# One decoder layer on one core: the next group's Gram products moved to the head of a body, the substitution moved ahead of the row scaling and scatter, and the long filter laced with the first inverse

## The chip, the cores and the metric

The kernel runs on one core of one Trainium2 chip. The metric is the device time of one execution in microseconds (us): 1143.61 is the median of three runs before the change (1141.53 to 1147.48).

## The reference

A pre-norm decoder layer in float32 over x of 4 x 1024 x 256: gated delta-rule attention, cross attention to 64 context rows, and a mixture of experts with a shared expert. Cut to what the change touches, the attention is:

```
hs = layernorm(x)
q, k, v = silu(causal_conv4(hs @ W))          # 4 heads of 64
A  = strict_lower((beta k) k^T)               # per chunk of 32 rows
u, w = inv(I + A) v, inv(I + A) (beta k)      # unit-triangular solve
for each chunk:                               # state S, 64 x 64 per head
    u = u - w S;  o = q S + lower(q k^T) u;  S = S + k^T u
short, long = fir3(v), fir31(v)
gates = softmax(gelu([hs, mean short, mean long, mean delta] W1) W2 / temp)
o = g0 short + g1 long + g2 delta + g3 v
x = x + (o * rsqrt(mean(o*o)) * w) @ Wo
x = x + cross_attention(layernorm(x), context)
x = x + moe(layernorm(x))                     # top 2 of 8 experts
```

The kernel solves blocks of 128 rows, not of 32: it inverts 32-row blocks by substitution and doubles them twice with products.

## The kernel before

The 4096 rows are eight groups of 512 (`NG`), a group four tiles of 128 (`T`), with 16 blocks of head and tile (`HT`). Each of the five engines has a program of its own, written out by hand in the order in which it runs: PE (TensorE) from L408, ACT (ScalarE) from L1033, POOL (GpSimd) from L1383, DVE (VectorE) from L1619, SP (which issues most DMAs) from L2332. Semaphores tie them together. An engine runs its queue strictly in order, so a wait holds back all that stands behind it. The eight PSUM banks go from one fill to the next: `open_bank` (L334) waits until the bank's last fill has been drained.

**Projection**: for each group PE projects six chunks, ACT evacuates them, DVE runs the four taps of the convolution (L1673) and lays v out for the long filter (`spread`, L1680).

**Long filter**: two channels of eight blocks on PE (`long_filter`, L492), ACT evacuates, DVE transposes each channel (`long_turned`, L1767) and SP stores it.

**Eight bodies** (`body`, PE L747, ACT L1239, POOL L1557, DVE L2005). Body i works on three things at once:

- the attention of group i. The inverse of its unit-triangular blocks is finished by products (`pair_inner`, L676; `pair_corner`, L687; `half_inner`, L702; `half_corner`, L713). `solved_rows` (L726) applies it, and two of the four resulting banks are copied by ACT, two by DVE (L2034). Then come the state loop (`wa`, masked by DVE at L2059 and L2063), the output loop (`outputs`), the gates (`gate_hidden`, L816, and the logits at L909, softmax on DVE from L2109), the mixing (L2137 to L2145), the output norm and the output products (L934);
- the cross attention and routing of group i-1, tagged x. DVE computes the row statistics (L1637, L1641), POOL their rstd (`norm_scale`, L1412: twice a body), DVE the normalised rows (`rows3`, L1647);
- the front of group i+1: Gram products (`front_gram` on PE, L468, a product pair for each of two banks of a tile, masked on DVE at L1722 and L1725), POOL's copies of the diagonal blocks (`front_diagonals`, L1442), DVE's transposition of them (`front_units`, L1732), POOL's substitution (`front_steps`, L1538: 31 steps, k = 31 down to 1, two operations each, L1544 and L1546), POOL's scaling of keys and values (`front_rows`, L1513 and L1516 for each tile), DVE's copies of the solved blocks (L1784, L1790).

From body 2 on, POOL also scatters the rows of group i-2 to the slots of the experts, two indirect DMAs a tile (L1489), each tile's behind the scaling of that tile. Their slots come from the positions that PE counts (`positions(i-2, 7)`, in bank 7) and DVE turns into slots (`slots`, from L1947).

POOL's order in a body is first `norm_scale`, all four tiles of `front_rows` with scatter, `front_solve` with the diagonals, and the steps, with two things between them:

```
                    if k == 18 and x is not None:
                        norm_scale(1, "x", 2 * x + 2)
                    if k == 5:
                        norm()
```

where `norm` is `output_norm` (L1558, one power of 128x8 for each half). Behind the bodies the tiles of the mixture of experts run; the change does not touch them.

## Time and profile before

| | |
|---|---|
| runs | 1143.61, 1147.48, 1141.53 us |
| the profiled execution | 1144.12 us, span 1142.3 us, mean granted clock 0.95 |
| PE busy | 997.4 us, 87% of the span |
| DVE busy | 803.6 us, 70% |
| POOL busy | 622.9 us, 55% |
| ACT busy | 528.2 us, 46% |

The span is the time from the first to the last instruction of the profiled execution; the rest of its own time lies around it. Busy is an average over stages: the projection takes until about 181 us, the long filter until about 217, the bodies from there until about 940, the tiles of the experts the rest. The granted clock is a share of TensorE's full 2.4 GHz. Rows give the start in us, the duration, the engine and its line, the operation, output and input, shapes, the count, and in brackets the idle time before it on that engine with what ended it.

### The profile page before, as it was taken

What the parts mean: (1) busy time and instruction counts of PE and PEld (TensorE: products, weight loads), DVE (VectorE), ACT (ScalarE), POOL (GpSimd) and SP (SyncE); (2) the same over time, 40 slices, a digit from 0 to 9 for tenths busy, and PEclk for the clock granted to TensorE, in tenths of its full rate; (3) what the DMA queues carried; (4) which work ended last, traced back from release to release, by engine and by line L of the source; (5) the groups of instructions that cost most, each with busy time, mean ns of one, the idle gap of its engine ahead of it and who ended that gap; (6) DMA issues with size and microseconds to landing.
All of it is one profiled execution on the core that took longest, in us unless ns stands there. A gap on an engine that the chain in (4) does not pass through costs nothing.

```text
span 1142.3 us, 26147 instructions
## 1 busy us (share of the span) xinstructions
PE 997.4 (87%) x9538; PEld 733.1 (64%) x9538; DVE 803.6 (70%) x2110; ACT 528.2 (46%) x992; POOL 622.9 (55%) x1009
## 2 busy tenths in 40 slices
PE   4899997887699899899999989989989999988991
PEld 2465657765476676576666667667667667767891
DVE  2879984543676866787677687687678775657487
ACT  2877774513333532542443443353253255755770
POOL 5469898438126636816816735653673215335562
PEclk9999998869799989999989999999999999999996
DMA  9444534450101250260161152122111173224589
GB/s 197 133 163 143 175 93 149 151 157 19 57 20 42 75 151 21 65 185 31 65 183 38 47 141 93 48 70 77 38 55 58 56 266 110 90 89 128 166 286 341
DMA packets 87100, 127.69 MB, mean 112 GB/s; under 512 B 28352, under 2 KB 62784, under 8 KB 84800
## 3 DMA queue, kind: packets, MB, share of 16 engines
q1 hardware_dynamic: 79776, 106.30, 30.2%
q0 software_dynamic: 7200, 19.74, 4.8%
q8 instruction: 78, 1.28, 0.5%
q14 instruction: 46, 0.38, 0.1%
HBM read 66.47 MB, written 59.55 MB: 110 GB/s over the span
## 4 chain that ended last, share of the span: by engine, by line
PE 45%; POOL 20%; DVE 20%; issue 8%; ACT 4%; DMA 1%; SPq 1%; ACTq 0%; DVEq 0%; POOLq 0%
POOL arena L1544 7%; POOL arena L1546 7%; DVE arena L1673 3%; PE bank L562 3%; PE bank L499 3%; PE bank L734 3%; PE bank L468 2%; PE bank L970 2%; POOL orn L1562 2%; PE bank L816 2%; POOL arena L1434 2%; PE bank L576 2%; PE bank L436 2%; PE bank L934 2%; PE bank L588 2%
## 5 line engine op out<-in xcount | busy, mean ns | idle before, releaser
L1044 ACT ACTIVATE arena<-bank 128x512 f32<-128x512 f32 (+4 forms) x358 | 185.9, 539 | 348.8 <-PE bank L961 61.8
L1544 POOL TENSOR_TENSOR arena<-arena 128x126 f32<-128x126 f32 (+22 forms) x248 | 107.0, 432 | 43.9 <-DVE arena L1732 26.1
L1673 DVE SCALAR_TENSOR_TENSOR arena<-arena,param 128x512 f32<-128x512 f32 x144 | 104.1, 777 | 18.8 <-ACT arena L1067 18.1
L1607 POOL DMA_INDIRECT results<-arena x78 | 76.3, 978 | 71.2 <-DVE arena L2225 42.9
L1546 POOL TENSOR_TENSOR arena<-arena 128x126 f32<-128x126 f32 (+22 forms) x248 | 102.2, 412 | 19.4
L419 PE MATMUL bank<-const,arena 128*128 128x128 f32 x256 | 40.5, 310 | 52.7 <-DVE arena L2162 26.7
L1489 POOL DMA_INDIRECT slots_x<-arena x64 | 63.6, 994 | 37.3 <-DVE arena L1964 21.4
L970 PE MATMUL bank<-arena 128*128 128x128 f32 x624 | 83.6, 277 | 0.2 <-ACT arena L1344 0.2
L1513 POOL TENSOR_TENSOR arena<-arena,rb 128x256 f32<-128x256 f32 x32 | 19.7, 616 | 116.5 <-ACT arena L1044 116.0
L970 PEld LDWEIGHTS bank<-arena 128*128 128x128 f32 x624 | 76.9, 194 | 0.4 <-issue 0.4
L1442 POOL COPY arena<-arena 32x128 f32<-32x128 f32 x128 | 53.5, 418 | 38.2 <-DVE arena L1722 31.4
L419 PEld LDWEIGHTS bank<-const,arena 128*128 128x128 f32 x256 | 33.2, 160 | 62.1 <-DVE arena L2162 29.7
L1722 DVE SCALAR_TENSOR_TENSOR arena<-bank,sc,const 128x128 f32<-128x128 f32 x128 | 38.5, 342 | 29.9 <-PE bank L468 29.9
L648 PE MATMUL bank<-arena 128*128 128x512 f32 x128 | 58.2, 608 | 0.0
L977 PE MATMUL bank<-arena 128*128 x156 | 49.5, 399 | 10.0 <-DVE arena L2214 9.8
L2214 DVE TENSOR_TENSOR arena<-bank,arena 128x128 f32<-128x128 f32 x78 | 22.3, 287 | 45.9 <-PE bank L970 23.6
L1854 DVE TENSOR_REDUCE top<-bank 128x8 f32<-128x512 f32 x64 | 43.8, 685 | 14.9 <-PE bank L579 14.7
L1275 ACT ACTIVATE wt<-bank 64x128 f32<-64x128 f32 x64 | 17.4, 271 | 74.0 <-PE bank L851 69.9
L1434 POOL TENSOR_SCALAR arena<-xt,mv_hs,rstd_hs 128x256 f32<-128x256 f32 x32 | 49.8, 1565 | 0.8
L1344 ACT ACTIVATE arena<-arena 128x512 f32 x78 | 48.7, 624 | 0.3
L468 PE MATMUL bank<-kq 64*128 64x256 f32 x224 | 35.5, 438 | 13.4 <-DVE arena L1725 12.3
L436 PE MATMUL bank<-hsT,wt 128*128 128x512 f32 x96 | 46.5, 628 | 0.8 <-ACT hsT L1044 0.8
(293 smaller groups left out, 2635.6 us busy)
## 6 DMA issues: line engine op xcount, KB each, us to landing
arena<-slots_x SPq DMA_DIRECT2D x78, 129.0 KB, 2.1
slots_x<-rows_of_no_token SPq DMA_DIRECT2D x8, 1161.0 KB, 11.7
xt<-x_in SPq DMA_DIRECT2D x16, 512.0 KB, 5.6
kq<-kq_T SPq DMA_DIRECT2D x8, 1024.0 KB, 9.0
arena<-results SPq DMA_DIRECT2D x32, 256.0 KB, 4.8
kq_T<-kq SPq DMA_DIRECT2D x7, 1024.0 KB, 3.9
arena<-ffn_in SPq DMA_DIRECT2D x7, 768.0 KB, 4.1
vT<-v_T SPq DMA_DIRECT2D x8, 514.0 KB, 4.0
```

What stands on the lines that cost most here:

```text
L419: last = tr(o[:, t * P:(t + 1) * P], src[:, t, c * P:(c + 1) * P], ident)
L436: last = mm(o[:, :], wgt("kqv"[j // 2], c, D)[:, (j % 2) * P:(j % 2 + 1) * P], hsT_b[i % 2][:, c, :], start=c == 0, stop=c == CK - 1)
L468: last = mm(o[r][:, c * 2 * P:(c + 1) * 2 * P], src[rr, c, 0, tt], src[rr, c, :, tt], start=True, stop=True)
L648: last = mm(o[:, :], w_[:, c, :], xnT[:, c, :], start=c == 0, stop=c == CK - 1)
L970: last = mm(o[:, s_ * P:(s_ + 1) * P], gu_w[:, n % 2, s_, c, :], xTs[:, n % 2, c, :], start=c == 0, stop=c == CK - 1)
L1044: free(act.activation(out_, in_, func, **kw), name)
L1434: done(pool.tensor_scalar(xn_hs[:, t, :], xt[:, i % G, t, :], mv[0][:, t, 0:1], rstd[0][:, t:t + 1], ALU.subtract, ALU.mult), "hs_rows_ready")
L1489: pool.indirect_dma_start(slots_x[PART[i]][:, :], bass.IndirectOffsetOnAxis(ap=slot_at[:, i * T + t, k:k + 1], axis=0), xn_f[:, t, :], Non ...
L1544: own.link(pool.tensor_tensor(tmp, rows32[:, m0:, k].unsqueeze(2).broadcast_to([P, nm, k]), units[:, 0:k, k].unsqueeze(1).broadcast_to([P, ...
L1546: ins = pool.tensor_tensor(rows32[:, m0:, 0:k], rows32[:, m0:, 0:k], tmp, ALU.subtract)
L1607: pool.indirect_dma_start(results[:, :], bass.IndirectOffsetOnAxis(ap=dest[:, n % YS:n % YS + 1], axis=0), ys[:, n % YS, :], None).then_in ...
L1673: ins = V.scalar_tensor_tensor(cv[:, k % 4, :], pre[:, j, d:d + GT], param[:, at:at + 1], cv[:, k % 4, :], ALU.mult, ALU.add)
```

## The change

- **Projection of the last group.** Its chunks run in the order 0, 4, 5, 1, 2, 3, so that v is there first; `spread(7)` follows the taps of its fifth chunk. The sums of squares of the last group move into the long filter.
- **Long filter and first inverse.** The long filter's second channel has storage of its own and uses three banks in turn. Its blocks alternate on PE and ACT with group 0's `pair_inner`, value tiles, `pair_corner`, `half_inner`, `half_corner`, and then with group 1's four Gram tiles. DVE masks those Gram tiles and transposes their units before body 0, POOL runs group 1's substitution before body 0.
- **Body 0** begins with `solved_rows(0)`. DVE's transposition of the second channel stands inside it. POOL does the output norm first and `front_rows(1)` behind it; group 1's value tiles stand at the end of PE's and ACT's body 0.
- **Bodies 1 to 6.** PE's Gram products of group i+1 stand before and behind `half_corner` (tiles 0 and 1, banks 6 and 7) and behind the second and third `wa` (tiles 2 and 3, banks 2 and 3); DVE's masks before its first scores, and behind the second and third `wa`; `front_units` behind the fourth. ACT copies all four banks of `solved_rows`.
- **POOL in bodies 1 to 6** runs diagonals and steps first. One tile of `front_rows` with its scatter follows each of the steps k = 28, 24, 20 and 16; the second `norm_scale` follows step 8 (it was 18); the output norm follows the last step (it was behind step 5).
- **SP** loads keys and queries of group i+2 in body i, the first `load_hs` earlier, and fills empty slots later; five loads of filter taps go with each group (it was four).

The core of the diff:

```diff
@@ POOL
-            def front_steps(i, x=None, norm=lambda: None):
+            ROWS_AT = (28, 24, 20, 16)
+
+            def front_steps(i, x=None, moved=None):
...
-                    if k == 18 and x is not None:
+                    if x is not None and k in ROWS_AT:
+                        front_rows(i, moved, (ROWS_AT.index(k),))
+                    if k == 8 and x is not None:
                         norm_scale(1, "x", 2 * x + 2)
-                    if k == 5:
-                        norm()
...
                 if i == 0:
-                    front_solve(1)
-                    front_steps(1)
+                    output_norm()
                     front_rows(1)
                 elif ahead:
-                    front_rows(i + 1, moved)
-                    if i >= 2:
-                        h = PART[i - 2]
-                        pool.wait_ge(sem(f"scattered{h}"), 32 * T * (i - 1 - FIRST[h]))
                     front_solve(i + 1)
-                    front_steps(i + 1, x, output_norm)
...
+                    for t in range(T):
+                        front_diagonals(i + 1, t)
+                    front_steps(i + 1, x, moved)
+                    output_norm()
@@ PE, body
                     queries()
...
+                    if ahead:
+                        keys_loaded(i + 1)
+                        next_gram(i + 1, 0, (6, 7))
+                    half_corner(i)
+                    if ahead:
+                        next_gram(i + 1, 1, (6, 7))
                     masked_scores(0)
...
                     if x and t == 1:
+                        if ahead:
+                            next_gram(i + 1, 2, (2, 3))
                         values(0)
@@ DVE, body
+                    if ahead:
+                        front_gram(i + 1, 0)
+                        front_gram(i + 1, 1)
                     scores(0)
-                    solved_rows()
...
                 if x:
+                    if ahead:
+                        filled(dve, f"edge1.{i}")
+                        front_units(i + 1)
                     scores(2)
@@ PE, ahead of body 0
+            pair_inner(0)
+            long_filter(1, 0)
+            front_values(0, 0)
+            pair_corner(0)
+            long_filter(1, 1)
...
+            for t in range(T):
+                next_gram(1, t)
                 long_filter(1, 4 + t)
```

Three places in the engines' orders, before and now. The first is POOL's queue at the head of a body before: `orn` is the output norm's result, `rstd_x` the x stream's rstd, `rb` and `sc` the factors of the scaling, the DMA is the pair of scatters of a tile, L1442 the diagonals, and the 128x31 operations the first step.

```order
L1414 TENSOR_TENSOR rstd_x<-mv_x,eps 128x4
L1415 TENSOR_TENSOR rstd_x<-rstd_x,minus_half 128x4
L1513 TENSOR_TENSOR arena<-arena,rb 128x4x64
L1516 TENSOR_TENSOR arena<-arena,sc 128x4x64
L1489 DMA slots_x<-arena 32768x258 x2
...
L1527 COPY arena<-start 128x512
L1442 COPY arena<-arena 32x32x4 x16
L1544 TENSOR_TENSOR arena<-arena 128x31
L1546 TENSOR_TENSOR arena<-arena 128x31
```

All four tiles of scaling and scatter (one shown) stood ahead of the diagonals and of the first step. Around the second rstd (behind the 128x126 step) and the output norm POOL's queue before was:

```order
L1546 TENSOR_TENSOR arena<-arena 128x7x18
L1414 TENSOR_TENSOR rstd_x<-mv_x,eps 128x4
L1415 TENSOR_TENSOR rstd_x<-rstd_x,minus_half 128x4
L1544 TENSOR_TENSOR arena<-arena 128x136
...
L1546 TENSOR_TENSOR arena<-arena 128x14x5
L1562 TENSOR_TENSOR orn<-oss,minus_half 128x8 x2
L1544 TENSOR_TENSOR arena<-arena 128x56
```

The same queue now, from the head of the body, with the first scaled tile, the rstd and the output norm.

```order
L1571 COPY arena<-start 128x512
L1486 COPY arena<-arena 32x32x4 x16
L1583 TENSOR_TENSOR arena<-arena 128x31
...
L1585 TENSOR_TENSOR arena<-arena 128x2x28
L1557 TENSOR_TENSOR arena<-arena,rb 128x4x64
L1560 TENSOR_TENSOR arena<-arena,sc 128x4x64
L1533 DMA slots_x<-arena 32768x258 x2
L1583 TENSOR_TENSOR arena<-arena 128x81
...
L1585 TENSOR_TENSOR arena<-arena 128x12x8
L1458 TENSOR_TENSOR rstd_x<-mv_x,eps 128x4
L1459 TENSOR_TENSOR rstd_x<-rstd_x,minus_half 128x4
...
L1601 TENSOR_TENSOR orn<-oss,minus_half 128x8 x2
```

The scaled tile and its scatter moved from ahead of the diagonals to between the steps, the rstd from behind the 128x126 step to behind the 128x96 step, the output norm to the end. The third place is PE's queue before, from the products of the queries (L562) to the half-corner (L723), the first scores (L576, L579) and the solved rows (L734):

```order
L562 MATMUL bank6<-arena,wt 128x512 x2
L723 MATMUL bank2<-arena 64x64 x8
L723 MATMUL bank3<-arena 64x64 x8
L576 MATMUL bank4<-arena 128x256
L576 MATMUL bank5<-arena 128x256
L576 MATMUL bank4<-arena 128x256
L576 MATMUL bank5<-arena 128x256
L579 MATMUL bank4<-mb,ident_b 128x512
L579 MATMUL bank5<-mb,ident_b 128x512
L734 MATMUL bank0<-arena 128x128 x4
```

and now, with the Gram products at L477 and the half-corner at L731:

```order
L570 MATMUL bank6<-arena,wt 128x512 x2
L477 MATMUL bank6<-kq1 128x256
L477 MATMUL bank7<-kq1 128x256
L477 MATMUL bank6<-kq1 128x256
L477 MATMUL bank7<-kq1 128x256
L731 MATMUL bank2<-arena 64x64 x8
L731 MATMUL bank3<-arena 64x64 x8
L477 MATMUL bank6<-kq1 128x256
L477 MATMUL bank7<-kq1 128x256
L477 MATMUL bank6<-kq1 128x256
L477 MATMUL bank7<-kq1 128x256
L584 MATMUL bank4<-arena 128x256
```

Two Gram tiles (four rows each) moved in, in banks 6 and 7; bank 6 holds the queries' second product just before.

## Rows read from the trace of the kernel before

**Rows 1.** The page: its first line, and the chain's shares by engine.

```profile
span 1142.3 us, 26147 instructions
...
PE 45%; POOL 20%; DVE 20%; issue 8%; ACT 4%; DMA 1%; SPq 1%; ACTq 0%; DVEq 0%; POOLq 0%
```

**Rows 2.** The timeline of POOL in body 3.

```profile
509.59 0.61 POOL L1513 TENSOR_TENSOR arena<-arena,rb 128x256 f32<-128x256 f32 x1 [17.79 <-ACT arena L1044]
...
513.32 0.62 POOL L1513 TENSOR_TENSOR arena<-arena,rb 128x256 f32<-128x256 f32 x1
...
539.27 0.25 POOL L1544 TENSOR_TENSOR arena<-arena 128x31 f32<-128x31 f32 x1 [3.92 <-DVE arena L1732]
...
552.34 0.20 POOL L1414 TENSOR_TENSOR rstd_x<-mv_x,eps 128x4 f32<-128x4 f32 x1
...
564.21 0.70 POOL L1546 TENSOR_TENSOR arena<-arena 128x96 f32<-128x96 f32 x1
...
567.81 3.23 POOL L1562 TENSOR_TENSOR orn<-oss,minus_half 128x8 f32<-128x8 f32 x2
```

**Rows 3.** The timeline of DVE in body 3.

```profile
502.24 0.18 DVE L1947 TENSOR_TENSOR arena<-bank,arena 128x32 f32<-128x32 f32 x1
...
507.41 0.69 DVE L2038 COPY arena<-bank 128x512 f32<-128x512 f32 x1 [0.20 <-PE bank L734]
...
518.26 0.57 DVE L2063 TENSOR_TENSOR wt<-const,bank 64x128 f32<-64x128 f32 x2
...
522.61 0.60 DVE L1722 SCALAR_TENSOR_TENSOR arena<-bank,sc,const 128x128 f32<-128x128 f32 x2
...
524.31 0.24 DVE L1865 RECIPROCAL rden<-bank 128x16 f32<-128x16 f32 x1
...
537.88 1.24 DVE L1732 STREAM_TRANSPOSE arena<-arena 128x1024 f32<-128x1024 f32 x1
...
553.77 2.14 DVE L1647 TENSOR_SCALAR arena<-xt,mv_x,rstd_x 128x256 f32<-128x256 f32 x4 [2.12 <-POOL rstd_x L1415]
...
574.49 1.06 DVE L1784 STREAM_TRANSPOSE arena<-arena 128x512 f32<-128x512 f32 x1 [0.35 <-POOL arena L1546]
```

**Rows 4.** The timeline of PE, from the end of body 2 to the end of body 3.

```profile
486.51 1.99 PE L934 MATMUL bank<-wt,arena 128*128 128x256 f32 x8
...
500.12 2.07 PE L723 MATMUL bank<-arena 64*64 64x64 f32 x32
...
524.53 1.13 PE L468 MATMUL bank<-kq 64*128 64x256 f32 x8 [1.14 <-DVE arena L1725]
...
578.15 1.99 PE L934 MATMUL bank<-wt,arena 128*128 128x256 f32 x8
```

**Rows 5.** The timelines of DVE and PE at the end of body 7.

```profile
916.43 1.39 DVE L1647 TENSOR_SCALAR arena<-xt,mv_x,rstd_x 128x256 f32<-128x256 f32 x4 [1.51 <-POOL rstd_x L1415]
...
935.69 3.62 PE L934 MATMUL bank<-wt,arena 128*128 128x256 f32 x16
```

**Rows 6.** The timelines of DVE and PE in bodies 0 and 1.

```profile
281.98 4.21 DVE L2141 SCALAR_TENSOR_TENSOR arena<-arena,gw 128x256 f32<-128x256 f32 x2
...
287.69 0.86 DVE L2141 SCALAR_TENSOR_TENSOR arena<-arena,gw 128x256 f32<-128x256 f32 x2
...
294.27 1.97 PE L419 MATMUL bank<-const,arena 128*128 128x128 f32 x8 [15.94 <-DVE arena L2162]
...
302.04 1.99 PE L934 MATMUL bank<-wt,arena 128*128 128x256 f32 x8
...
368.55 2.21 DVE L1647 TENSOR_SCALAR arena<-xt,mv_x,rstd_x 128x256 f32<-128x256 f32 x4 [2.02 <-POOL rstd_x L1415]
```

**Rows 7.** Windows: stretch, length, busy time by engine, PEclk, DMA share, GB/s.

```profile
496.88:518.83 21.95, 21.92 (x259) 17.17 (x259) 17.95 (x42) 8.72 (x15) 8.09 (x11) 1.00 0.46 138
217.80:245.20 27.40, 17.56 (x192) 13.75 (x192) 14.37 (x32) 7.42 (x13) 6.72 (x32) 0.53 0.73 241
294.00:301.00 7.00, 6.00 (x29) 4.44 (x31) 2.08 (x4) 3.59 (x6) 0.00 (x0) 0.50 0.01 2
```

More of the change, by code:

```diff
@@ L778, in body @@
                 for t in range(T):
-                    if ahead:
+                    if x and ahead:
                         front_values(i + 1, t)
@@ L818, in gate_hidden, with head_means @@
                         full(last, n)
-                n = f"gm.{i}"
-                o = open_bank(pe, n, next(body_bank))
-                pe.wait_ge(sem("short_done"), 2 * i + 2)
-                pe.wait_ge(sem("long_loaded"), 16 * (i + 1))
-                for c in range(CK):
-                    mm(o[0:DH, :], cst("mean_s")[:, 0:DH], sht[:, c, :], start=c == 0, stop=c == CK - 1)
-                    last = mm(o[DH:2 * DH, :], cst("mean_l")[:, DH:2 * DH], lng[:, c, :], start=c == 0, stop=c == CK - 1)
-                full(last, n)
-                if x and ahead:
-                    next_gram(i + 1, 1)
+                def head_means():
+                    n = f"gm.{i}"
+                    o = open_bank(pe, n, next(body_bank))
+                    pe.wait_ge(sem("short_done"), 2 * i + 2)
+                    pe.wait_ge(sem("long_loaded"), 16 * (i + 1))
+                    for c in range(CK):
+                        mm(o[0:DH, :], cst("mean_s")[:, 0:DH], sht[:, c, :], start=c == 0, stop=c == CK - 1)
+                        last = mm(o[DH:2 * DH, :], cst("mean_l")[:, DH:2 * DH], lng[:, c, :], start=c == 0,
+                                  stop=c == CK - 1)
+                    full(last, n)
+                if x:
+                    head_means()
                 pe.wait_ge(sem("hs_loaded"), 16 * (i + 1))
@@ L834, in body @@
                 for t in range(T):
-                    if x and ahead and t == 0:
-                        next_gram(i + 1, 2)
                     drained(pe, f"wa{t}.{i}")
@@ L1094, in _ @@
             for i in range(NG):
-                for j in range(3):
-                    project(i, j)
+                for k in range(3):
+                    project(i, k)
                 if i:
@@ L1223, in solved_rows @@
             def solved_rows(i):
-                for t in range(T // 2):
+                for t in range(T):
                     n = f"solve{t}.{i}"
@@ L1255, in body @@
                 for t in range(T):
-                    if ahead:
+                    if x and ahead:
                         front_values(i + 1, t)
@@ L1509, in front_rows @@
                 kvi = kvt[i % 2]
-                for t in range(T):
+                for t in ts:
                     drained(pool, f"kv{t}.{i}")
@@ L1591, in _ @@
             front_rows(0)
-            drained(pool, "long07")
-            pool.memset(Tf, 0.0).then_inc(setup_main, 1)
+            front_solve(1)
+            for t in range(T):
+                front_diagonals(1, t)
+            front_steps(1)
             pool.wait_ge(sem("long_ready"), CK * NG)
@@ L1747, in _ @@
                     spread(i - 1)
-                for j in range(1, 6):
-                    tap(i, j, 1)
-                    tap(i, j - 1, 3)
-                    tap(i, j, 2)
-                    if j == 2 and 3 <= i < 3 + T:
+                for k in range(1, 6):
+                    tap(i, k, 1)
+                    tap(i, k - 1, 3)
+                    tap(i, k, 2)
+                    if k == 2 and 3 <= i < 3 + T:
                         front_gram(0, i - 3)
+                    if k == 4 and i == NG - 1:
+                        spread(i)
                 if i == 2 + T:
@@ L1759, in _ @@
                     halo(i + 1)
-            spread(NG - 1)
             def later_scales():
@@ L2097, in body @@
                     outputs(t)
-                    if x and ahead and t == 1:
-                        front_units(i + 1)
+                    if not x and t < FS:
+                        short_filter((t,))
                     if x and t == 1:
```

294 lines of the change are left out of this document (159 added, 135 removed).

## The prediction

> **What bounds the kernel now.** I read the page first, for the chain that ended last: TensorE (PE) holds 45% of it, GpSimd (POOL) and VectorE (DVE) 20% each [rows 1]. No engine is the bound all through, so what counts is which wait ends last at each place. Then I read the timelines of one body in the middle, body 3. Its start m is where the last output product of body 2 ends, 486.51 + 1.99 = 488.50, and its end is the same product one body later, 578.15 + 1.99 = 580.14 [rows 4]: a period of 91.64 us.
>
> In that body POOL scales and scatters four tiles, one every 513.32 − 509.59 = 3.73 us, then starts the substitution at S = 539.27, which is m + 50.8 [rows 2]. In the middle of its steps it computes the second rstd of the other stream (the one row-normalisation `rows3` waits for): it begins at 552.34, as soon as the statistics are there, for DVE's `rows3` at 553.77 (m + 65.3) names POOL as its releaser after 2.12 us of idling [rows 2, 3]. The output norm (3.23 us at 567.81) also stands between the steps, and DVE's copy of the solved blocks at 574.49 waited only 0.35 us for POOL's last step [rows 2, 3]. The reader should see that POOL is **just in time at three places**: rstd, output norm and last step. Whatever makes one of them later moves the body's end.
>
> **The order on POOL.** The change lets POOL begin earlier, but puts more in front of the rstd. To the end of step k = 8 the steps run from 539.27 to 564.21 + 0.70 = 564.91, and 553.77 − 552.34 = 1.43 of that is the rstd itself, which leaves 24.2 us of steps [rows 2, 3]. Four tiles of scaling and scatter, 4 × 3.73 = 14.9 us, now stand among the steps before k = 8 instead of before S. So `rows3` can start at S + 24.2 + 14.9 + 1.4 = S + 40.5, where it now starts at S + 14.5. DVE's queue is strictly in order: behind `rows3` stand the gate's softmax, the mixing, the output norm's sums, and with them everything to the body's end. The change pays only as far as S comes earlier, and needs 26 us of it.
>
> **How early S can be.** S follows the transposition of the units (1.24 us at 537.88 [rows 3]), now right behind the last of four masks of the state loop, which DVE ended at 518.26 + 0.57 = 518.83.
> - Lower bound, DVE's work alone. Ahead of it come four Gram tiles at 524.31 − 522.61 = 1.70 each, 6.8 in all; two bank copies of 0.69 go to ScalarE (ACT), −1.4 [rows 3]. Between 496.88 and 518.83 DVE was busy 17.95 of 21.95 us [rows 7]; if the new work takes all of that gap, −4.0. 518.83 + 6.8 − 1.4 − 4.0 + 1.24 = 521.5, m + 33.0.
> - Upper bound. The Gram products of the first tile use a bank that holds the positions of the group before the last, which DVE empties only at 502.24 + 0.18 [rows 3]. The products (1.13 a tile; 524.53 shows PE itself waiting 1.14 for DVE to empty a Gram bank) then end near 503.6, and the half-corner products that began at 500.12 stand behind them: +3.4 [rows 4]. With DVE's four tiles in series and a copy of 0.69 more on ACT: 518.83 + 3.4 + 6.8 + 0.7 + 1.24 = 531.0, m + 42.5.
> - I take 528.7, **m + 40.2**: PE's three other tiles cost 3.4, the last tile's 1.7 on DVE is open, half of the last copy and 1.24 follow. It is nearer the upper end because each tile is a chain PE, DVE, PE on two banks, as the wait in rows 4 shows.
>
> `rows3` then starts at m + 80.7 instead of m + 65.3: **+15.4** (from +8.2 to +17.7).
>
> **The tail behind it.** From `rows3` to the end of the last product is 580.14 − 553.77 = 26.4 us now. In body 7, where POOL has no substitution, it is 935.69 + 3.62 − 916.43 = 22.9 [rows 5]; the compaction of 1.06 us [rows 3] and the next group's first inverse products are missing there. With POOL idle beside it the new tail should be like body 7's: from 23.9 (with the compaction) to 26.4; I take 24.8, −1.6. The output norm that now follows all steps costs nothing: from k = 8 on POOL has some 6 us of steps, and the sums come some 14 us after `rows3`. If that cover were gone, 3.23 us would come back per body.
>
> TensorE's clock speaks here too. At the end of body 0 PE idled 15.94 us before 294.27 [rows 6], and in 294 to 301 its granted clock was 0.50, the 1.2 GHz level, while it was busy 6.00 of 7 us [rows 7]. PE would idle for a similar time before `rows3`, so up to 3.0 us per body may be lost; most of PE's work behind `rows3` is not on DVE's path, so the sum has 0 for it. The Trainium skill, "TensorE: Matmul & The Clock Gate" (Part 1), says that the slow level is the default and activity releases it: by that rule the full 3.0 us would come in each such body, the case "clock" below; the row at 294 agrees with the rule.
>
> **Bodies 2 to 6**: 5 × (15.4 − 1.6) = +69. **Body 1** has no scatter, so a tile costs only the two products of 0.61 [rows 2], 4.8 in all. But four value tiles of the next group now stand ahead of its first inverse copies, each about a copy of 0.69 with its products in front; between 2.8 and 7 us, I take 5.2. Its S is m + 45.4 and `rows3` at m + 45.4 + 24.2 + 4.8 + 1.4 = m + 75.8; now it is 368.55 − (302.04 + 1.99) = m + 64.5 [rows 6]. +11.3 − 1.6 = +9.7.
>
> **The start.** The 27.4 us from 217.8, the end of the long filter, to 245.2, where PE begins the first solved rows, have PE busy 17.56 at a granted clock of 0.53 [rows 7]. Laced between the long filter's blocks the same work would take 17.56 × 0.53 = 9.3: −18.1. Of that I take −15: the long filter's second transposition on DVE moves into body 0 and part of it may delay the state loop. In body 0, the mixing product at 281.98 took 4.21 for two, the next pair 0.86 [rows 6]; POOL's scaling of group 1 ran beside it, and is now behind the output norm: −3.4. Together **−18.4** (from −10 to −24). The other loads, bank cycle and chunk order I cost at nothing: they stand under the projection and long filter, where PE never waits for a load. Body 7: all four copies on ACT, +1.
>
> **Sum.** −18.4 + 9.7 + 69 + 1 = +61.3. The profiled execution took 1144.1 us (span 1142.3 [rows 1]); that gives 1205.4, and as it lies 0.5 over the median of the runs shown, **1205**. All ends low: 5 × (8.2 − 2.5) + 1 − 24 = +5.5, 1149; all high, with the clock: 5 × (17.7 + 1.4) + 15 − 10 + 1 = +101.5, 1245.
>
> **The rivals.**
> - *Faster: POOL does not bind.* It decides at one point: if S ≤ m + 24.8, the rstd is ready by m + 65.3 as now. Then −18.4, the tail's −1.6 six times, +5 for the value tiles: 1121. For it: POOL idles long before its first tile in each body. Against it: DVE's own work puts S at m + 33.0 or later. Chance 0.07.
> - *The Gram work sinks into idle time.* S at the lower bound, +8.2 − 1.6 in five bodies, +3 in body 1, −18.4 + 1: +19, 1163. For it: DVE idles 4 us there. Against it: PE's wait for the positions' bank. 0.15.
> - *Clock.* As forecast, with 3.0 us more in six bodies: 1223. For it the window at 294. Against it: part of that work has slack. 0.27.
> - *No difference.* Start's gain and bodies' loss cancel; that needs S near m + 29, also below DVE's work. 1144. 0.04.
> - The forecast itself: 0.47.
>
> **The numbers.** About 0.5% is what a measurement of this kernel can tell from no change. Faster 0.07, same 0.04, slower the rest, 0.89. The range takes in the sunken Gram work, the clock and the bounds of S except their last ends: 1160 to 1235.
>
> **What would show it.** In bodies 2 to 6 `rows3` idles some 14 us for POOL's rstd, and that rstd stands behind the 128 × 96 step, near m + 79; the period is near 105; the output norm waits for DVE's sums; solved rows of group 0 near 228 to 230; S near m + 40. If `rows3` starts at about m + 65 with no long idle, the step "S + 40.5" is wrong; if S is under m + 33, the DVE count is.

## The result and the profile after

The changed kernel takes 1217.42 us (median of four runs, 1217.08 to 1221.63) against 1143.59 before: the ratio is 1.0648, 95% interval [1.0624, 1.0672]. The forecast was 1205 within 1160 to 1235, so the time lies in the range and 12.4 us above the forecast. The profiled execution has a span of 1215.9 us, 73.6 us more than before.

The page after, its first line, PE's and the other engines' busy time, and the granted clock in 40 slices:

```profile
span 1215.9 us, 26194 instructions
...
PE 1014.9 (83%) x9538; PEld 753.2 (62%) x9538; DVE 783.7 (64%) x2095; ACT 537.1 (44%) x1008; POOL 614.6 (51%) x1008
...
PEclk9899989977999997898889789988978999999996
```

POOL and DVE are busy for less time than before. ACT has 8.9 us more, for it now copies all four banks of the solved rows. PE's 17.5 us more are as many products (9538) at a lower mean clock (0.919, it was 0.95). So little of the 73.6 us is additional work; most of the loss is waiting. Stage by stage (a body's start m is, as in the prediction, the end of the last output product of the body before it; the last column is an experiment that is told below):

| us | before | forecast | after | difference | with both fillers |
|---|---|---|---|---|---|
| start, to m of body 1 | 304.03 | −18.4 | 287.44 | −16.6 | −17.7 |
| body 1 | 91.94 | +9.7 | 97.77 | +5.8 | +5.9 |
| bodies 2 to 6 | 461.08 | +69 | 541.67 | +80.6 | +60.4 |
| body 7 | 82.26 | +1 | 86.53 | +4.3 | +1.1 |
| behind it | 202.99 | 0 | 202.49 | −0.5 | +0.3 |
| sum | 1142.3 | +61.3 | 1215.9 | +73.6 | +50.0 |

The timeline of POOL in body 3 (m = 491.37), to be held beside [rows 2]:

```profile
534.89 0.25 POOL L1583 TENSOR_TENSOR arena<-arena 128x31 f32<-128x31 f32 x1 [1.64 <-DVE arena L1774]
...
539.47 1.08 POOL L1533 DMA_INDIRECT slots_x<-arena  x1 [0.17 <-issue]
...
573.44 0.20 POOL L1458 TENSOR_TENSOR rstd_x<-mv_x,eps 128x4 f32<-128x4 f32 x1
...
579.89 0.23 POOL L1585 TENSOR_TENSOR arena<-arena 128x16 f32<-128x16 f32 x1
...
586.74 1.65 POOL L1601 TENSOR_TENSOR orn<-oss,minus_half 128x8 f32<-128x8 f32 x1 [6.16 <-DVE oss L2192]
```

The substitution starts at S = m + 43.5 (it was m + 50.8), the rstd follows 38.55 us later, and the output norm idles 6.16 us for DVE's sums: POOL is early for the norm and far too late for the rstd. DVE in the same body, beside [rows 3]:

```profile
505.44 0.18 DVE L1990 TENSOR_TENSOR arena<-bank,arena 128x32 f32<-128x32 f32 x1
...
533.50 1.25 DVE L1774 STREAM_TRANSPOSE arena<-arena 128x1024 f32<-128x1024 f32 x1
...
560.51 0.28 DVE L1682 BATCH_NORM_AGGREGATE mv_x<-stats_x 128x2 f32<-128x6 f32 x3
...
574.87 1.74 DVE L1688 TENSOR_SCALAR arena<-xt,mv_x,rstd_x 128x256 f32<-128x256 f32 x4 [14.08 <-POOL rstd_x L1459]
...
588.05 0.69 DVE L1943 TENSOR_TENSOR arena<-bank,arena 128x512 f32<-128x512 f32 x1 [1.39 <-PE bank L656]
```

The statistics are ready at 560.79; `rows3` idles 14.08 us for the rstd that POOL computes behind its k = 8 step, as forecast. In bodies 2 to 6 this wait is 14.1 to 15.2 us. By the last line DVE, in the tail, waits 1.39 us for PE. PE in body 3, from the last product of body 2 to that of body 3, beside [rows 4]:

```profile
489.38 1.99 PE L940 MATMUL bank<-wt,arena 128*128 128x256 f32 x8
...
505.77 1.25 PE L477 MATMUL bank<-kq 64*128 64x256 f32 x8 [2.71 <-DVE arena L1990]
506.95 3.68 PE L731 MATMUL bank<-arena 64*64 64x64 f32 x32
510.56 2.08 PE L477 MATMUL bank<-kq 64*128 64x256 f32 x8
...
576.66 1.97 PE L428 MATMUL bank<-const,arena 128*128 128x128 f32 x8 [11.45 <-DVE arena L1688]
...
582.70 7.03 PE L656 MATMUL bank<-arena 128*128 128x512 f32 x16
...
597.72 1.99 PE L940 MATMUL bank<-wt,arena 128*128 128x256 f32 x8
```

and the windows (columns as in [rows 7]: stretch, length, busy time of PE, PEld, DVE, ACT and POOL, granted clock, DMA share, GB/s) behind PE's two waits, and at the start of body 7:

```profile
506.00:514.50 8.50, 8.50 (x60) 6.93 (x59) 4.36 (x18) 1.18 (x2) 1.80 (x5) 0.60 0.18 62
...
576.00:583.00 7.00, 6.34 (x33) 6.23 (x34) 5.49 (x22) 4.26 (x8) 3.71 (x13) 0.59 0.00 1
...
926.90:936.50 9.60, 8.92 (x156) 7.50 (x157) 8.56 (x30) 4.65 (x9) 1.21 (x2) 0.83 0.19 58
```

Before, body 3 ran at 1.00 here, from m + 8.4 on [rows 7]. Now PE waits 2.71 us for DVE to empty the positions' bank, and behind that wait it runs at a mean of 0.60, mostly the 1.2 GHz level: the half-corner takes 3.68 us where it took 2.07 [rows 4], a Gram tile 2.08 instead of 1.13. Behind the 11.45 us that PE waits for `rows3` it is 0.59. The fall at the head does not follow every such wait. In body 2 of the same execution PE waits 2.36 us at the same place, and the stretch behind it is at 1.00:

```profile
401.41 1.13 PE L477 MATMUL bank<-kq 64*128 64x256 f32 x8 [2.36 <-DVE arena L1990]
402.48 2.08 PE L731 MATMUL bank<-arena 64*64 64x64 f32 x32
```

```profile
401.64:410.14 8.50, 8.50 (x88) 7.50 (x87) 6.90 (x21) 2.78 (x5) 3.18 (x8) 1.00 0.19 64
```

In bodies 3 to 6 the 8.5 us from m + 14.6 on are at 0.60 to 0.62, with a wait of 2.36 us in three of them. Three questions were left: what the rstd's place costs by itself, what the clock costs, and which part of the change is worth keeping.

### The profile page after: what moved, and what is told of

It is laid out like the page before. It is cut to its first block, busy times and chain, and to the rows that moved or that the text cites. A ratio compares the mean times of both kernels' runs of the same rounds, so it can differ in the third digit from the quotient of the medians.

```text
span 1215.9 us, 26194 instructions
## 1 busy us (share of the span) xinstructions
PE 1014.9 (83%) x9538; PEld 753.2 (62%) x9538; DVE 783.7 (64%) x2095; ACT 537.1 (44%) x1008; POOL 614.6 (51%) x1008
## 4 chain that ended last, share of the span: by engine, by line
PE 44%; POOL 21%; DVE 20%; issue 7%; ACT 6%; DMA 2%; ACTq 0%; SPq 0%; POOLq 0%; DVEq 0%
POOL arena L1583 5%; POOL arena L1585 4%; POOL slots_x L1533 3%; PE bank L428 3%; PE bank L477 3%; DVE arena L1715 3%; PE bank L570 3%; PE bank L507 3%; PE bank L940 3%; PE bank L656 3%; PE bank L742 2%; PE bank L990 2%; POOL arena L1478 2%; ACT arena L1064 2%; PE bank L445 2%
## 5 line engine op out<-in xcount | busy, mean ns | idle before, releaser
L1064 ACT ACTIVATE arena<-bank 128x512 f32<-128x512 f32 (+4 forms) x374 | 195.8, 542 | 382.3 <-PE bank L731 67.7
L428 PE MATMUL bank<-const,arena 128*128 128x128 f32 x256 | 44.9, 332 | 104.9 <-DVE arena L1688 63.2
L1583 POOL TENSOR_TENSOR arena<-arena 128x126 f32<-128x126 f32 (+22 forms) x248 | 103.6, 418 | 29.0 <-DVE arena L1774 12.0
L428 PEld LDWEIGHTS bank<-const,arena 128*128 128x128 f32 x256 | 36.0, 171 | 115.5 <-DVE arena L1688 65.0
L1585 POOL TENSOR_TENSOR arena<-arena 128x126 f32<-128x126 f32 (+22 forms) x248 | 96.8, 390 | 19.4
L1688 DVE TENSOR_SCALAR arena<-xt,mv_x,rstd_x 128x256 f32<-128x256 f32 x64 | 24.6, 445 | 84.4 <-POOL rstd_x L1459 84.4
L1601 POOL TENSOR_TENSOR orn<-oss,minus_half 128x8 f32<-128x8 f32 x16 | 26.2, 1643 | 66.9 <-DVE oss L2192 66.9
L1897 DVE TENSOR_REDUCE top<-bank 128x8 f32<-128x512 f32 x64 | 43.9, 686 | 22.9 <-PE bank L587 22.6
L656 PE MATMUL bank<-arena 128*128 128x512 f32 x128 | 58.2, 608 | 0.0
L2124 DVE TENSOR_TENSOR arena<-bank,rn 128x256 f32<-128x256 f32 x32 | 13.6, 425 | 62.7 <-PE bank L872 62.5
L2257 DVE TENSOR_TENSOR arena<-bank,arena 128x128 f32<-128x128 f32 x78 | 22.4, 288 | 44.8 <-PE bank L990 22.9
L477 PE MATMUL bank<-kq 64*128 64x256 f32 x224 | 35.6, 440 | 14.4 <-DVE arena L1990 12.2
```

The lines of the kernel that those rows point to most:

```text
L428: last = tr(o[:, t * P:(t + 1) * P], src[:, t, c * P:(c + 1) * P], ident)
L477: last = mm(o[r][:, c * 2 * P:(c + 1) * 2 * P], src[rr, c, 0, tt], src[rr, c, :, tt], start=True, stop=True)
L656: last = mm(o[:, :], w_[:, c, :], xnT[:, c, :], start=c == 0, stop=c == CK - 1)
L1064: free(act.activation(out_, in_, func, **kw), name)
L1583: own.link(pool.tensor_tensor(tmp, rows32[:, m0:, k].unsqueeze(2).broadcast_to([P, nm, k]), units[:, 0:k, k].unsqueeze(1).broadcast_to([P, ...
L1585: ins = pool.tensor_tensor(rows32[:, m0:, 0:k], rows32[:, m0:, 0:k], tmp, ALU.subtract)
```

## The experiments

Each ratio below is to runs of the kernel before on the same chip.

### The rstd back behind k = 18

```diff
-                    if k == 8 and x is not None:
+                    if k == 18 and x is not None:
                         norm_scale(1, "x", 2 * x + 2)
```

> The changed kernel with one number changed back: the second rstd stands behind step 18 again, not behind step 8. Theory P (rows3 waits for POOL, because the scaled tiles and scatters now stand among the steps ahead of the rstd): in bodies 2 to 6 POOL reaches step 18 at S + 13 + 3 x 3.7 = S + 24, about m + 68, the statistics come at m + 69, so rows3 starts near m + 71 instead of m + 83.5 and no longer idles for POOL. But POOL then ends its steps near m + 92, so the output norm now waits for POOL: the next body's end near m + 104, 4 us earlier, total near 1197. Theory G (the Gram products at the head are what costs, the rstd only happens to be late): rows3 moves but the period stays 108, 1217. Theory C (TensorE's slow clock behind the long idle is what costs): the idle is gone, the tail gets 3 us shorter, 1200 with no wait for POOL at the output norm.

Measured: 1195.05 us, ratio 1.046 [1.0409, 1.0512]. The total is what the theory of POOL's queue gave (1197), but not by the floor that it named. DVE's and POOL's timelines in body 3:

```profile
574.59 2.25 DVE L1688 TENSOR_SCALAR arena<-xt,mv_x,rstd_x 128x256 f32<-128x256 f32 x4 [8.98 <-DMA slots_x<-arena]
```

```profile
566.03 1.04 POOL L1459 TENSOR_TENSOR rstd_x<-rstd_x,minus_half 128x4 f32<-128x4 f32 x1
...
571.99 0.96 POOL L1533 DMA_INDIRECT slots_x<-arena  x1 [0.30 <-issue]
```

The rstd is there at 567.07, and `rows3` starts 7.5 us later, released by a scatter. `rows3` overwrites the buffer from which the scatters read, and so waits for the last of them to land. Scatters spread among the steps are thus a **second floor** under `rows3`: m + 75.4 to m + 79.1 in bodies 2 to 6, where the rstd's place gave m + 82.1 to m + 84.4. The prediction did not see it; in the changed kernel it does not bind, since the rstd comes later still. In body 1, which has no scatter, `rows3` comes at m + 73.5, and there DVE waits 4.4 us for the output norm, which now stands behind all steps: the cover that the prediction named for it is gone as soon as the rstd is early.

### The half-corner ahead of both Gram tiles

```diff
+                    half_corner(i)
                     if ahead:
                         keys_loaded(i + 1)
                         next_gram(i + 1, 0, (6, 7))
-                    half_corner(i)
-                    if ahead:
                         next_gram(i + 1, 1, (6, 7))
```

> The changed kernel with half_corner ahead of both Gram tiles, so that it no longer stands behind the wait for bank 7. Theory W (PE's wait of 2.7 us for bank 7 is what sets TensorE's clock down to the 1.2 GHz level behind it, which makes S 3.3 us later than forecast): the half-corner products take 2.1 us instead of 3.7, the granted clock of the stretch behind stays near 1.0, S comes near m + 40, the total near 1200. Rival (the clock falls there for another reason, or the Gram tiles' own wait takes over): S stays at m + 43, total within 4 us of 1217.

Measured: 1216.44 us, ratio 1.0648 [1.0591, 1.0705]: no difference to the change. The sum hides two movements. In bodies 2 to 6 the wait for the positions' bank shrinks (0.35 us in body 3, with the half-corner at 2.07), and they are 5.1 us shorter together. But a new wait of 1.94 us, for DVE's masks, stands before the second Gram tile; the clock falls elsewhere, to 0.72 in 512 to 515; and S still comes at m + 40.5 to m + 44.5. Body 1 is 8.0 us longer (105.75); body 7, 3.2 us shorter, makes up for part of it. The window of body 1's head:

```profile
300.00:310.00 10.00, 9.81 (x47) 6.68 (x46) 4.68 (x9) 3.54 (x6) 0.00 (x0) 0.50 0.01 2
```

and that of the changed kernel, whose body 1 starts 1.1 us earlier, at the full clock:

```profile
300.00:310.00 10.00, 9.36 (x79) 6.15 (x77) 7.76 (x16) 3.34 (x7) 0.00 (x0) 1.00 0.01 2
```

Both had idled alike just before (PE busy 8.00 and 8.01 of the 12 us from 288). This run alone can't weigh the head's order: the place at which the clock falls moved with it, and took the gain of the new order back. Why it moved is not shown.

### The start alone

The bodies get their old order back (Gram products, solved rows, POOL's order); the lacing of the long filter, the projection's order, the loads and body 0 stay changed.

```diff
-                    front_steps(i + 1, x, moved)
-                    output_norm()
+                    front_rows(i + 1, moved)
...
+                    front_steps(i + 1, x, output_norm)
```

> Only the start of the change: long filter laced with the first inverse, group 1's front ahead of body 0, body 0 as changed, the SP order; bodies 1 to 7 in the order of before. The parts add up (my theory): the start's gain of 16.6 us stays and the bodies' loss goes: 1125 to 1131, faster than before. Rival (the start's gain only moves a wait, body 1 gives it back since its value tiles and first inverse come late): 1140 or more.

Measured: 1141.0 us, ratio 0.998 [0.995, 1.0009]: the parts do not add up, and the total is the rival's. In the profiled execution body 1 starts at 287.01, 17.0 us earlier, but 7.3 of that are given back in body 1 (99.21 us; it was 91.94). That execution took 1135.08 us. Of the ten, three took 1134 to 1135 and seven 1140 to 1145; what the seven lose beyond that no profile shows. DVE's timeline there:

```profile
294.91 1.38 DVE L1686 TENSOR_SCALAR arena<-xt,mv_x,rstd_x 128x256 f32<-128x256 f32 x4 [5.24 <-POOL rstd_x L1459]
```

Its first normalised rows wait 5.24 us for an rstd that stands on POOL's queue behind `front_rows(1)`; and that waits for the value tiles that the change put at the end of body 0. The changed kernel has the same wait (5.16 us), so body 1's price was only partly the one in the prediction.

### The start, mended

On top of the last kernel, the value tiles of group 1 use four banks instead of one, ACT copies them behind body 1's first inverse, and POOL scales group 1 behind body 1's first rstd.

```diff
-                o = open_bank(pe, n, 7)
+                o = open_bank(pe, n, (7, 4, 5, 6)[t] if i == 1 else 7)
...
+                if i == 1:
+                    front_rows(1)
```

> The start alone (as in the run of that name), with what body 1 gave back mended: POOL scales group 1's rows behind body 1's first rstd instead of ahead of it, its four value tiles go to four banks instead of one, and ACT copies them behind the first inverse products. Theory (body 1 lost 7 us because POOL's rstd stood behind the scaling, which waited for the value tiles): the first x rows of body 1 start 3.5 us behind the body's start instead of 7.9, the profiled execution near 1129, 6 us under the start alone and some 14 under before. Rival (body 1 is late for the slow clock alone): within 2 us of the start alone.

Measured: 1131.82 us, ratio 0.9875 [0.9846, 0.9904]. The rows wait 0.67 us for POOL, as in the kernel before, and body 1 takes 93.05 us, 6.2 less than in the start alone; bodies 2 to 6 are 2.8 us longer together, which was not followed up. Once body 1 doesn't wait, the start is worth 16.4 us up to m of body 1 (18.4 were forecast, within −10 to −24), and 13.1 in the median of the whole kernel.

### Scatter ahead of the steps, scaling behind them

```diff
                     for t in range(T):
                         front_diagonals(i + 1, t)
+                        if moved is not None and t < 2:
+                            scatter(moved, (2 * t, 2 * t + 1))
...
                     output_norm()
+                    front_rows(i + 1)
```

The tiles of `front_rows` no longer stand among the steps, so that neither floor is left. (The scatters, two tiles at a time, are waited for on POOL ahead of the steps.)

> The changed kernel with POOL's order changed: the scatters of the group before the last between the diagonals (POOL idles there), the scaling of the four tiles behind the output norm; nothing but steps ahead of the rstd, which stays behind step 8. Theory P: rows3 starts at S + 24 + 1.4, or with the statistics, near m + 71 instead of m + 83.5, the output norm does not wait for POOL, the period is near 96 instead of 108.3, total near 1150. Theory G (Gram at the head costs): period stays over 105, total over 1200.

Measured: 1173.93 us, ratio 1.0292 [1.0238, 1.0346]. DVE in body 3:

```profile
549.68 1.75 DVE L1686 TENSOR_SCALAR arena<-xt,mv_x,rstd_x 128x256 f32<-128x256 f32 x4 [1.58 <-POOL rstd_x L1459]
...
565.82 1.09 DVE L2197 TENSOR_TENSOR arena<-arena,orn 128x512 f32<-128x512 f32 x1 [0.54 <-POOL orn L1597]
```

The wait of 14.08 us is down to 1.58 us, and 43.5 of the 73.8 us are gone (what the clock loses behind that wait among them): that POOL's queue ahead of the rstd is the main cost, is shown. But 1150 was expected. The period is 93.8 to 101.3 us and not 96. The tail is longer (25.8 to 28.0): POOL's scaling now runs beside DVE's last products (1.09 us, where the same product took 0.68 just before the scaling began), and in body 3 PE's last output product, behind a wait of 1.44 us for DVE, takes 3.49 us instead of 1.99. And S is at m + 41.7 to m + 47.8: in the stretch of 8.5 us from m + 14.6 on the granted clock was 1.00 in bodies 2 and 3, and 0.53 to 0.66 in bodies 4 to 6.

### Both reorderings

The last kernel with the half-corner ahead of both Gram tiles.

> The early scatters and the half-corner first together. If PE's wait at the head delays the row statistics too, which now decide rows3, the period of 100 falls by 2 to 3 us and the total to about 1160; if the clock's falls decide, it stays near 1172.

Measured: 1164.07 us, ratio 1.0167 [1.0129, 1.0205]; periods of 94.9 to 98.3 us. The move that alone took 5.1 us off bodies 2 to 6 and nothing off the total takes 12.1 off these bodies here, and 9.9 off the median. The granted clock of the stretch from m + 14.6 on is 0.69 to 1.00 in the five bodies (0.53 to 1.00 without the move; 1.00 in body 3 of both), and S is at m + 41.2 to m + 44.7. How much of the gain is the order and how much the clock, is not shown. In the old order the period is 91.7 to 92.5 (the start alone), so even in its best order here the middle of the change costs 4.4 us a body (96.6 against 92.2 in the mean).

### A busy PE at the tail

The dummy products below are additional work: they write to a bank that the next fill clears, and nothing reads them. They only keep PE busy where it waits.

```diff
+                    if i >= 2 and ahead:
+                        for _ in range(19):
+                            mm(banks[2][:, :], wt[:, 0:P], wt[:, 0:4 * P], start=True, stop=True)
```

> The changed kernel with 19 products of 128x512 into an unused bank in PE's 11 us of idling ahead of rows3 in bodies 2 to 6 (about 10.5 us of work that nothing needs), so that only the idling goes, not the wait. Theory C (the slow clock behind the idling costs time on the path): the granted clock behind rows3 stays near 1.0 instead of 0.59, the products there take 1.04 instead of 1.97, the tail of 24.8 us gets 2 to 3 us shorter, total near 1204. Rival (those products have slack, as the forecast assumed): tail and total stay, 1217 within 4.

Measured: 1224.04 us, ratio 1.0691 [1.065, 1.0732]. PE's timeline in body 3:

```profile
574.22 16.47 PE L921 MATMUL bank<-wt 128*128 128x512 f32 x38
```

This run did not decide. The clock stayed at 1.00, but a 128x512 product in float32 is two instructions, 38 of 16.47 / 38 = 0.43 us, and the filler ended at 590.69, though `rows3` had started at 584.08: PE's own work came late. With 12 products instead of 19:

> The changed kernel with 12 products that nothing uses (128x512, into bank 2) ahead of the normalised rows' transposition in bodies 2 to 6, in place of the 19 of the busy tail. 19 took 16.47 us and ran 4.6 us into the tail; 12 should take about 10.4 us and fit into PE's idle 11.45 us. If PE's clock behind the wait for rows3 is on the path (the case 'clock'), the granted clock there is 1.00 instead of 0.59, the tail 2 to 3 us shorter than 24.8 and the time 1203 to 1208. If PE's work behind rows3 has slack, as the forecast's sum has it, the tail stays at 24 to 25 and the time at 1215 to 1219.

Measured: 1205.02 us, ratio 1.0549 [1.0515, 1.0584]. PE in body 3 (m = 491.28):

```profile
564.96 10.47 PE L921 MATMUL bank<-wt 128*128 128x512 f32 x24
576.58 1.09 PE L428 MATMUL bank<-const,arena 128*128 128x128 f32 x8 [1.15 <-DVE arena L1691]
...
580.47 7.03 PE L656 MATMUL bank<-arena 128*128 128x512 f32 x16
```

and its window behind the wait:

```profile
575.00:582.00 7.00, 5.78 (x37) 4.38 (x37) 5.74 (x22) 3.65 (x8) 4.49 (x15) 1.00 0.00 1
```

The transposition takes 1.09 us instead of 1.97, the hidden products of L656 begin at 580.47 instead of 582.70, and DVE's wait for them is gone. The tail is 22.8 to 24.0 us (22.8 or 22.9 in four of the five bodies), where it was 24.1 to 25.3. The slow clock behind `rows3` was on the path, at 2 us a body: the case "clock" and not the forecast's zero.

### A busy PE at the head

```diff
                     if ahead:
                         keys_loaded(i + 1)
+                        if i >= 2:
+                            for _ in range(5):
+                                mm(banks[2][:, :], wt[:, 0:P], wt[:, 0:4 * P], start=True, stop=True)
                         next_gram(i + 1, 0, (6, 7))
```

> The changed kernel with 5 products of 128x512 into a free bank in PE's wait of 2.7 us for bank 7 at the head of bodies 2 to 6; the wait itself stays. Theory C (the wait lets the clock fall, and the clock makes the half-corner and Gram products slow): granted clock of the next 8 us near 1.0 instead of 0.60, half corner 2.1 instead of 3.7, S near m + 40.5 instead of m + 43.5, total near 1202. Rival (the clock falls there anyway, as it did elsewhere when the half-corner stood first): S stays, 1217 within 4.

Measured: 1209.92 us, ratio 1.0567 [1.0528, 1.0607]. The five products took 4.45 us and ran 1.7 us past the wait that they fill, and still the kernel was 7.5 us faster than the change. With three:

> The busy head with 3 such products instead of 5 ahead of each body's first Gram tile: 2.6 us, which fits into PE's wait of 2.71 us for DVE to empty the positions' bank, where 5 ran 1.7 us past it. If the fall of the granted clock at that wait is what put S over the forecast's upper bound of m + 42.5, then the half-corner stays at 2.1 us, S comes at m + 40 to m + 42, and the time is 1200 to 1209, no later than the busy head's 1209.9. If the wait itself or the order of PE's queue did it, S stays at m + 43.5 and the time at 1217.

Measured: 1203.72 us, ratio 1.0533 [1.0505, 1.056]. PE in body 3 (m = 491.19):

```profile
502.73 2.74 PE L772 MATMUL bank<-wt 128*128 128x512 f32 x6
505.60 1.14 PE L477 MATMUL bank<-kq 64*128 64x256 f32 x8
506.66 2.08 PE L731 MATMUL bank<-arena 64*64 64x64 f32 x32
508.67 1.13 PE L477 MATMUL bank<-kq 64*128 64x256 f32 x8
```

and its window:

```profile
506.00:514.50 8.50, 8.50 (x89) 7.51 (x86) 6.72 (x20) 2.96 (x5) 3.16 (x8) 1.00 0.19 64
```

The first Gram tile starts at 505.60, as early as without the filler (505.77), and everything behind it runs at the full clock: 3.68 − 2.08 for the half-corner, 2.08 − 1.13 for the Gram tile and 0.5 for the scores make 3.1 us, and S comes at m + 40.4, 3.1 us earlier. In all five bodies that stretch is now at 1.00. A wait of 2.71 us cost more in what followed it than it lasted. (The profiled execution, 1200.6 us, is the shortest of the four.)

### Both fillers

```diff
+                            for _ in range(3):
...
+                        for _ in range(12):
```

> The changed kernel with both fillers, 3 products ahead of each body's first Gram tile and 12 ahead of the normalised rows' transposition, in bodies 2 to 6. Alone they took 13.7 and 12.4 us off the changed kernel's 1217.4; about 3.0 us of each (body 7's start) is the same gain. If the two falls of the clock cost time independently, S comes at m + 40 to m + 41, the tail is near 22.8, a body of 2 to 6 lasts 102.5 to 104 us and the time is 1217.4 - 13.7 - 12.4 + 3.0 = 1194, between 1191 and 1198. If one fall hands the same time on to the other (a body's head is slow because its predecessor's tail was), the gain together is that of the larger alone, 1203 to 1205.

Measured: 1194.31 us, ratio 1.0453 [1.0421, 1.0485], where the single gains, with body 7's 3.0 us counted once, make 1217.4 − 13.7 − 12.4 + 3.0 = 1194.3. The windows of the two stretches of body 3 (m = 489.22), as far behind m and behind the start of `rows3` as in the changed kernel:

```profile
503.85:512.35 8.50, 8.50 (x88) 7.50 (x87) 6.88 (x21) 2.79 (x5) 3.17 (x8) 1.00 0.17 62
570.69:577.69 7.00, 6.27 (x38) 4.76 (x39) 5.73 (x23) 4.56 (x10) 3.73 (x13) 1.00 0.00 1
```

So the two falls cost time independently (the interval is some 4 us wide on either side, so the agreement to a tenth is luck), and together they are worth 1217.4 − 1194.3 = 23.1 us of the 73.8 that the change loses. The other 50.7 are the rest of the change taken together: POOL's order, the place of the Gram products and body 1, less the start's gain. No run takes these apart with both fillers in. Nor is 23.1 all that a lower clock costs: the first 9.6 us of bodies 2, 4 and 6 are still at 0.77 in this run, and before the change they were at 0.73 or 0.74.

### The units one step earlier

On the mended start, DVE transposes the units behind the first `outputs` and not the second. POOL's rstd moves two steps back and its output norm one (k counts down), so that both keep about their old time; the expectation's "earlier" is a slip of words, for among the steps they stand later.

```diff
-                    if k == 18 and x is not None:
+                    if k == 16 and x is not None:
...
-                    if k == 5:
+                    if k == 4:
...
-                    if x and ahead and t == 1:
+                    if x and ahead and t == 0:
```

> The mended start with DVE's transposition of the units one step earlier (behind the first outputs instead of the second) and POOL's second rstd and output norm correspondingly earlier in its steps (behind k = 16 instead of 18, and behind k = 4 instead of 5). If POOL's start is what bodies of the old order wait for, S comes some 2.5 us earlier and a body is 1.1 to 1.5 us shorter: 1122 to 1126 against 1131.8. If DVE's own queue bounds the middle of the body, the transposition only changes places and the time stays within 1129 to 1134.

Measured: 1121.73 us, ratio 0.98 [0.977, 0.9829], the fastest kernel of the study, 2% below the one before. POOL's and DVE's timelines in body 3 (m = 471.18):

```profile
519.47 0.25 POOL L1581 TENSOR_TENSOR arena<-arena 128x31 f32<-128x31 f32 x1 [1.43 <-DVE arena L1773]
```

```profile
536.11 2.11 DVE L1687 TENSOR_SCALAR arena<-xt,mv_x,rstd_x 128x256 f32<-128x256 f32 x4 [1.62 <-POOL rstd_x L1459]
```

In body 3 S is at m + 48.3, 2.5 us earlier than in the mended start, as expected. `rows3` is only 0.3 us earlier there (m + 64.9), and the tails of bodies 1 to 6 are 25.2 to 25.9 us, where the mended start has 26.3 to 27.4. Bodies 1 to 6 are 7.6 us shorter together. Another 2.9 us lie behind body 7, where the two kernels have the same instructions; where these come from was not tried. The aim of the change, an earlier substitution, was right in these bodies: it paid here, where nothing was put in front of the rstd for it.

## Why the prediction was right

**The mechanism: right.** The change puts four tiles of scaling and scatter ahead of the rstd and gains only part of it back at S. From S to `rows3` the prediction had 40.5 us; measured are 40.0 (574.87 − 534.89). The rstd stands behind the 128 x 96 step, at m + 82.1 in body 3 (forecast near m + 79; S was later), the wait is 14.1 to 15.2, the output norm waits for DVE's sums, and the copy of the solved blocks no longer waits for POOL. The rival "POOL does not bind" needed S at m + 24.8 or earlier; no kernel came near it. "The Gram work sinks into idle time" needed m + 33.0; S was at m + 39.5 at the earliest.

**S: mis-sized.** The step that failed is the term "I take 528.7, m + 40.2" with its upper bound of m + 42.5: S was at m + 42.2 to m + 44.4, in four of five bodies above the bound. The order of the work was foreseen, the wait for the positions' bank with it, at 3.4 us. What the bound left out is the clock behind that wait. The one body inside the bound, body 2, is the one whose clock stayed at 1.00 behind it. With the wait filled S is at m + 40.4 in body 3, 0.2 from the value taken, and between 39.5 and 42.3 in the others. (The parts named for 528.7, with the 3.4 of the wait, add up to 518.83 + 3.4 + 3.4 + 1.7 + 0.35 + 1.24 = 528.9; the difference decides nothing.)

**The tail: right by two errors that cancel.** Forecast 24.8, measured 24.84 in body 3 and 24.1 to 25.3 in bodies 2 to 6. The prediction made it from body 7's 22.9, the compaction, and no cost of the clock. With the clock at 1.00 the tail is 22.8, body 7's own value: the compaction shows no cost there, and the clock costs 2.0 us. That the time came out right here was luck. The sentence "most of PE's work behind `rows3` is not on DVE's path, so the sum has 0 for it" was wrong, and so was the case "clock" in its size, 3.0 us in six bodies; it also had only one of the two places. The clock cost 2 us a body in the tails, 2 to 3 in the heads (S at m + 43.5 in the mean of the five bodies, 41.5 with both fillers, 40.6 with the head's alone), and 3.0 once in body 7 (its start at 0.83 after, 1.00 before and with either filler).

**Bodies 2 to 6.** 80.6 against 69. With both waits filled it is 60.4: forecast and measurement differ by the clock (+20.2) and by −8.6 the other way, of which five tails of 22.8 instead of 24.8 make −9.8, S +6.5 (m + 41.5 in the mean of the run with both fillers) and the shorter stretch behind S −2.8. The rest is the base: body 3 (91.64 us) was one of the shorter of the bodies, whose mean is 92.2. One body in the middle stands for the others only within a microsecond, and the sum multiplies that by five. The clock is in this too. The first 9.6 us of bodies 4 and 5 before the change:

```profile
580.15:589.75 9.60, 8.40 (x145) 6.30 (x146) 6.95 (x24) 4.14 (x7) 1.21 (x2) 0.73 0.90 258
672.74:682.34 9.60, 8.73 (x159) 7.01 (x160) 9.14 (x31) 4.54 (x9) 1.21 (x2) 1.00 0.88 231
```

Bodies 2, 4 and 6 start at 0.73 or 0.74 and last 92.5 to 92.7 us, bodies 3 and 5 start at 1.00 and last 91.6. The body that the prediction read is one of the two without a slow stretch.

**Body 1 and the start.** Start −16.6 against −18.4. Body 1 +5.8 against +9.7. What the value tiles cost was taken as 5.2 us, and the wait they leave is 5.16 us in DVE's timeline of body 1:

```profile
295.27 1.67 DVE L1688 TENSOR_SCALAR arena<-xt,mv_x,rstd_x 128x256 f32<-128x256 f32 x4 [5.16 <-POOL rstd_x L1459]
```

but it comes by POOL's queue, not by ACT's copies ahead of the inverse: the size was met by luck, and the path was wrong. S is at m + 45.1 (forecast m + 45.4) and `rows3` at m + 74.6 (75.8); the rest of the difference is the tail, 23.2 instead of 25.8, at the full clock there.

POOL's scaling beside the mixing, forecast at −3.4 in body 0, went as told: the scaling of group 1 now begins only at 288.69. DVE's timeline of body 0, against 4.21 us in [rows 6]:

```profile
268.68 0.87 DVE L2178 SCALAR_TENSOR_TENSOR arena<-arena,gw 128x256 f32<-128x256 f32 x2
```

The Trainium skill, "SBUF — State Buffer" (Who interferes with whom), says that a DVE instruction with two inputs in SBUF contends with a GpSimd instruction that reads SBUF; this row, and the 1.09 us of the scatter-early run, agree.

**What the clock case should have been.** The Trainium skill, "TensorE: Matmul & The Clock Gate" (Part 1), has activity release the slow level. The two fillers agree with it in this kernel: the same products at the same places run at 0.60 and 0.59 behind an idle PE and at 1.00 behind one that did useless work. Body 1 of the corner-first run does not (busy 9.81 of 10.00 us at 0.50). The prediction cited the rule, and then applied it only to the long wait, not to the new short one that it had itself found; and the long one it took at nothing.

## What to carry to other kernels

When work is moved ahead on an in-order queue, cost it at the first consumer behind it on that queue, not at the work that gets earlier: here an S that came 7 us sooner cost 18 us at the rstd. Count every wait that the new order gives TensorE, short ones too, and price what runs behind it at both clock levels; a few useless products in the wait tell whether the clock is on the path. And test a large change by its parts: the start and a small shift of one transposition gave 2%, where the whole lost 6.5%.

## What was not expected of the hardware

- PE idled only 2.71 us behind 11.69 us in which it was busy for 10.89 at 1.00, and the granted clock of the 8.5 us behind it was 0.60, with PE busy throughout. Filled with 2.74 us of products, it was 1.00.
- The same wait was not always followed by a fall. In body 2 of the changed kernel, and in bodies 4 and 6 with the tail's filler alone, PE waited 2.36 us there and the stretch behind was at 1.00; the first 9.6 us of these bodies were at 0.73 to 0.78.
- A busy PE is not always a fast one: in body 1 of the corner-first run PE was busy 9.81 of 10.00 us at 0.50, behind about the same idling as in the changed kernel, where it ran at 1.00. Which small shift decides this stayed open.
- The first 9.6 us of body 7 ran at 0.83 in the changed kernel and at 1.00 with either filler alone, though the head's filler stands 90 us ahead of it in the sixth body. What carries over was not tried.
- A body's S alternates by 1.9 us (40.4, 42.3, 40.4, 42.2 in bodies 3 to 6 with both fillers); the kernel before has 1.0 (50.8, 51.7). The granted clock of the first 9.6 us goes with it: 0.77 in bodies 2, 4 and 6 with both fillers and 1.00 in 3 and 5; before, 0.73 or 0.74 and 1.00. What makes every other body start slow stayed open.
